# Two message-passing layers on one core: sums over partitions of two groups in four strips, and fewer waits

## The reference

```
h = 2.0 ** 0.5 * relu(emb @ W1 / 10.0 ** 0.5)                 # (E, 16)
w = (h @ W2 / 16.0 ** 0.5).reshape(E, 7, MUL, MOUT)           # 7 weight matrices per edge
s_out, g_out = 8 scalars each, from xs and xv.y1
v_out        = 8 vectors,      from xs, xv and xv.y2
s_act = 1.593 * tanh(s_out); gates = 1.593 * tanh(g_out)
edge_ftr = concat([s_act, gates[:, :, None] * v_out]) * norm[:, None]
return segment_sum(edge_ftr, edge_dst)
```

## Time and profile before

| | us |
|---|---|
| three executions | 5657.39, 5658.57, 5661.72 |
| median | 5658.57 |
| the profiled execution | 5663.47 |
| its span, first to last instruction | 5661.7 |
| message stage in it (first to last `FT` copy) | 416 to 3341 |

### The profile page before, as it was taken

One profiled execution on the slowest core, in us unless ns is written; L12 is line 12 of the kernel. 1 busy time (PEld: TensorE's weight loads), 2 busy tenths in 40 slices (PEclk: granted clock), 3 DMA queues, 4 the chain that ended last, 5 costly groups with the idle time before them and its releaser, 6 DMA issues. The chain is left out here.

```text
span 5661.7 us, 70210 instructions
## 1 busy us (share of the span) xinstructions
PE 4006.7 (71%) x20839; PEld 2129.7 (38%) x20839; DVE 3192.8 (56%) x5351; ACT 1475.9 (26%) x2862; POOL 3379.2 (60%) x3371
## 2 busy tenths in 40 slices
PE   0005888787888888877877860099898998999870
PEld 0002322222222222232222320077666666766650
DVE  4504776776767776677776763044444444455442
ACT  2002444444444444444444430000000000001000
POOL 5675555555555555555555417666666666666756
PEclk9999888888888888888888985599999989999985
DMA  8411111111111111111111101022222222222211
GB/s 300 114 38 18 38 37 36 37 37 37 37 35 33 36 37 31 34 37 37 37 37 37 35 18 22 18 41 45 43 43 43 42 43 43 43 42 48 46 27 24
DMA packets 266652, 252.42 MB, mean 45 GB/s; under 512 B 182208, under 2 KB 236936, under 8 KB 263777
## 3 DMA queue, kind: packets, MB, share of 16 engines
q1 hardware_dynamic: 157028, 174.83, 11.2%
q0 software_dynamic: 109024, 72.30, 9.0%
q10 hardware_dynamic: 462, 4.00, 0.2%
HBM read 160.54 MB, written 90.34 MB: 44 GB/s over the span
## 5 line engine op out<-in xcount | busy, mean ns | idle before, releaser
L612 POOL DMA_INDIRECT edge<-xp_d,idx x1440 | 1421.4, 987 | 1089.0 <-issue 419.4
L864 DVE TENSOR_TENSOR prod<-G_ps,hid 128x1000 f32<-128x1000 f32 x1200 | 1399.4, 1194 | 884.6 <-remote 410.6
L1198 POOL DMA_INDIRECT gxb<-tab_d,idxb x1200 | 1259.1, 1049 | 577.0 <-issue 334.4
L753 PE MATMUL G_ps<-FT,wst 32*128 32x500 f32 x4800 | 999.3, 685 | 362.7 <-DVE prod L864 244.4
L1233 PE MATMUL G_ps<-tb,hot 125*126 125x500 f32 (+1 forms) x3200 | 727.8, 378 | 395.5 <-DVE hotk L1255 301.1
L782 PE MATMUL R_ps<-prod,red 128*32 128x500 f32 x4800 | 923.8, 706 | 0.8 <-ACT rt L678 0.8
L1233 PEld LDWEIGHTS G_ps<-tb,hot 125*126 125x126 f32 x3200 | 572.0, 201 | 537.5 <-issue 446.8
L753 PEld LDWEIGHTS G_ps<-FT,wst 32*128 32x128 f32 x4800 | 270.7, 200 | 827.5 <-DVE prod L864 412.3
L773 PE MATMUL T_ps<-FT,wst 32*128 32x500 f32 x800 | 522.4, 737 | 3.1 <-issue 3.1
L666 ACT ACTIVATE FT<-T_ps 128x500 f32<-128x500 f32 x400 | 235.0, 588 | 856.3 <-PE G_ps L753 629.9
L782 PEld LDWEIGHTS R_ps<-prod,red 128*32 128x32 f32 x4800 | 180.8, 124 | 691.2 <-issue 445.5
(11 more groups left out here) (242 smaller groups left out, 4541.3 us busy)
## 6 DMA issues: line engine op xcount, KB each, us to landing
xd_d<-zeros SPq DMA_DIRECT2D x16, 1562.5 KB
y_d<-zrb SPq DMA_DIRECT2D x40, 595.0 KB
edge<-xp_d,idx POOLq DMA_INDIRECT x1440
xv<-xd_d SPq DMA_DIRECT2D x40, 560.0 KB
y_d<-zr SPq DMA_DIRECT2D x40, 560.0 KB
edge<-sel_d SPq DMA_DIRECT2D x40, 546.9 KB
gxb<-tab_d,idxb POOLq DMA_INDIRECT x1200
em<-in_edge_attr SPq DMA_DIRECT2D x40, 175.0 KB
```

Of the source, the lines that this page charges most:

```text
L612: nc.gpsimd.indirect_dma_start(out=edge_c[:, i, 8:8 + DIM], out_offset=None, in_=xp_d, in_offset=bass.IndirectOffsetOnAxis(col, 0)).then_i ...
L753: return Tn.matmul(G_ps[pair][:, a * 512:a * 512 + GW], wst[rows, r * 128:(r + 1) * 128], FT[k][rows, :], start=True, stop=True)
L864: V.tensor_tensor(prod[k][i][:, :].rearrange("p (a e) -> p a e", a=2), gv, hid[k][:, :].rearrange("p (a e) -> p a e", a=1).broadcast_to([1 ...
L1198: nc.gpsimd.indirect_dma_start(out=gx[h][:, c * T1:(c + 1) * T1], out_offset=None, in_=tab_d, in_offset=bass.IndirectOffsetOnAxis(idx[h][: ...
```

## The change

The sums over partitions are made per piece, not per group. Each of a piece's two groups has six pairs (product tile, half) to be added up; `sum_round` takes them in three rounds of four matmuls, each round filling four strips of 32 rows of `R_ps` (two strips per group). `out_of_R` copies 128 rows once per piece, and `back` makes four transposes of 128 rows per piece where there were eight of 96. `red` gets a third block, `prod` four sets of tiles (until now two), `rt` is one tile. The orders of the three engines around it move: on ScalarE `high` comes a group earlier, tanh and the copy of the sums go once per piece; on VectorE `post(0)` and `post(1)` come one group later and `turned` moves to the other group of the piece; transposes of features take columns alternately. A number of waits that another wait in the same stream implies are left out. On GpSimd the indices are copied per piece, and the wait for five ring slots before the copy is gone; `pace` is as it was.

```diff
-        red = sb("red", [128, 2 * 32])
+        red = sb("red", [128, 3 * 32])
...
-            prod = [[sbt(f"prod{k}_{i}", [128, 2 * GW]) for i in range(3)] for k in range(2)]
-            rt = [sbt(f"rt{k}", [96, GW]) for k in range(2)]
+            prod = [[sbt(f"prod{k}_{i}", [128, 2 * GW]) for i in range(3)] for k in range(4)]
+            rt = sbt("rt", [128, GW])
@@ -603,11 +604,9 @@
-                                if c == 0 and s % PC == 0 and not fixed:
-                                    for q in range(s, s + PC):
-                                        hold(S(f"b_gx{q}"), t * 16 * PW + 16 * PW)
-                                    nc.gpsimd.tensor_copy(idx[:, i:i + C], src_i[:, bass.ds((p + RING) * PW, C)]).then_inc(S("b_ix"), 1)
-                                    hold(S("b_ix"), t * 2 + s // PC - 1)
+                                if c == 0 and not fixed:
+                                    nc.gpsimd.tensor_copy(idx[:, i:i + PW], src_i[:, bass.ds((p + RING) * PW, PW)]).then_inc(S("b_ix"), 1)
+                                    hold(S("b_ix"), p - RING + 1)
@@ -687,11 +681,16 @@
-                            if k == 1 and not (last and g + 3 >= G2):
-                                s = (g + 3) // 2
+                            if k == 0 and not (first and g < 4):
+                                tanh(t * RING + g // 2 - 2)
+                            if k == 0 and not (last and g + 4 >= G2):
+                                s = (g + 4) // 2
                                 high(t * RING + s, s % RING, t * 2 + s // PC)
+                            if k == 1 and not (first and g < 2):
+                                out_of_R(t * RING + g // 2 - 1)
...
+                            if not (last and g == G2 - 1):
+                                relu(n + 1, 1 - k)
                             if not (last and g >= G2 - 2):
                                 out_of_T(n + 2, k)
-                            if k == 1 and not (first and g < 3):
-                                tanh(t * RING + (g - 3) // 2)
-                            if not (last and g == G2 - 1):
-                                relu(n + 1, 1 - k)
-                            if not (first and g == 0):
-                                out_of_R(n - 1, 1 - k)
@@ -772,40 +764,45 @@
-                    def reduce(n, k):
-                        pe.wait_ge(S("b_mul"), n * 3 + 3)
-                        if some(n):
-                            pe.wait_ge(S("b_rt"), n)
-                        for a in range(2):
-                            for o in range(3):
-                                i = (o, (0, 2, 1)[o])[a]
-                                last = Tn.matmul(R_ps[32 * o:32 * o + 32, 0:GW], red[:, a * KF:(a + 1) * KF], prod[k][i][:, a * GW:(a + 1) * GW], start=(a == 0), stop=(a == 1))
-                        last.then_inc(S("b_R"), 1)
...
+                    def sum_round(m, b, u):
+                        if u == 0:
+                            pe.wait_ge(S("b_mul"), m * 6 + 6)
+                            if some(m):
+                                pe.wait_ge(S("b_rt"), m)
+                        for q in range(4):
+                            pair, a = ((0, 0), (1, 0), (2, 0), (0, 1), (2, 1), (1, 1))[q % 2 * 3 + u]
+                            last = Tn.matmul(R_ps[32 * q:32 * q + 32, 0:GW], red[:, u * KF:(u + 1) * KF],
+                                             prod[b * 2 + q // 2][pair][:, a * GW:(a + 1) * GW], start=(u == 0), stop=(u == 2))
+                        if u == 2:
+                            last.then_inc(S("b_R"), 1)
+
+                    def back(m):
+                        pe.wait_ge(S("b_rt"), m + 1)
+                        if some(m):
+                            pe.wait_ge(S("b_yr"), m)
                         pe.sem_inc(S("go"), 1)
                         for c in range(GT):
+                            last = Tn.transpose(Y_ps[0:P, c * 128:(c + 1) * 128], rt[:, c * P:(c + 1) * P], ident[:, :])
                         last.then_inc(S("b_Y"), 1)
@@ -854,17 +852,17 @@
                         if i == 0:
                             dve.wait_ge(S("b_hid"), n + 1)
-                        dve.wait_ge(S("b_G"), n * 2 + (1, 1, 2)[i])
-                        if i == 0 and later(n):
-                            dve.wait_ge(S("b_R"), n - 1)
+                            dve.wait_ge(S("b_G"), n + 1)
+                        if i == 2:
+                            dve.wait_ge(S("b_G2"), n + 1)
...
-                            if k == 0:
-                                q = (g + 4) // 2
+                            if k == 1:
+                                q = (g + 5) // 2
                                 more = not (last and q >= RING)
                                 if more:
                                     turned(t * RING + q, q % RING, t * 2 + q // PC, q % RING // PC, t + q // RING)
...
-                            elif not (first and g < 3):
-                                q = (g - 3) // 2
+                            elif not (first and g < 4):
+                                q = (g - 4) // 2
                                 for i in range(2):
                                     post(i, t * RING + q, q % RING // PC, q % RING % PC, t if q >= 0 else t - 1)
```

More of the change, by code:

```diff
@@ L249, in _ @@
                     nc.gpsimd.memset(edge_c[:, :, SD + 40:EW], 0.0)
-                    for i in range(2):
+                    for i in range(3):
                         blk = red[:, i * KF + i * MO:i * KF + (i + 1) * MO]
@@ L648, in gather_sums @@
                         act.wait_ge(S(f"b_z{h}"), t * NPC + i + 1)
-                        if some(ch):
+                        if i == 0 and some(ch):
                             act.wait_ge(S("b_st"), ch * 32)
@@ L766, in round2 @@
                         product(k, 1, 0, 0, 0)
[L767 removed]
+                        product(k, 1, 1, 0, 1).then_inc(S("b_G2"), 1)
                     def hidden(n, k):
@@ L798, in turn @@
                             g2, p2 = (g + 2) % G2, t * RING + (g + 2) // 2
+                            m, b = t * RING + g // 2 - 1, (g // 2 - 1) % 2
+                            sums_due = not (first and g < 2)
                             round1(n, k)
+                            if sums_due:
+                                sum_round(m, b, 2 * k)
                             if not (last and g >= G2 - 2):
                                 transposes(n + 2, g2, p2)
-                            if not (first and g < 2):
-                                back(n - 2, k)
                             round2(n, k)
@@ L806, in turn @@
                                 hidden(n + 1, 1 - k)
-                            if not (first and g == 0):
-                                reduce(n - 1, 1 - k)
+                            if sums_due and k == 0:
+                                sum_round(m, b, 1)
+                            if sums_due and k == 1:
+                                back(m)
                     transposes(0, 0, 0)
@@ L816, in _ @@
                     turn(PAIRS - 1, last=True)
-                    reduce(NG - 1, 1)
-                    back(NG - 2, 0)
-                    back(NG - 1, 1)
+                    for u in range(3):
+                        sum_round(NPIECES - 1, 1, u)
+                    back(NPIECES - 1)
                 @block.vector
@@ L914, in turn @@
                                 scan = lambda: fill(gc, ch + 1, 1 - h)
[L915 to L920 removed]
+                            if 5 <= gc < 9 and not (first and h == 0):
+                                scan = lambda: sums(gc - 5, ch - 1, 1 - h)
+                            multiply(n, k, b, 0)
+                            multiply(n, k, b, 1)
+                            if k == 1 and not (first and g < 5):
+                                q = (g - 5) // 2
                                 post(2, t * RING + q, q % RING // PC, q % RING % PC, t if q >= 0 else t - 1)
@@ L951, in _ @@
                         fill(i, 0, 0)
-                    for p in range(2):
+                    for p in range(3):
                         turned(p, p, 0, 0, 0)
@@ L958, in _ @@
                     turn(PAIRS - 1, last=True)
-                    post(2, NPIECES - 2, 1, PC - 2, PAIRS - 1)
-                    for i in range(3):
-                        post(i, NPIECES - 1, 1, PC - 1, PAIRS - 1)
+                    for p in range(2):
+                        for i in range(3):
+                            post(i, NPIECES - 2 + p, 1, PC - 2 + p, PAIRS - 1)
                     carry_sums(NCH - 1, 1, PAIRS - 1)
```

77 lines of the change are left out of this document (30 added, 47 removed).

## The result

The changed kernel is slower: 5876.72 us (median of 4, 5875.1 to 5909.66) against 5660.15 for the kernel before on the same chip (5657.39 to 5674.17), a ratio of 1.0391, 95% interval 1.0351 to 1.0432. On another chip it was 1.0392 (1.0362 to 1.0422). The forecast was 5600, its range 5450 to 5800.

A forecast was written before the change was run, and what follows sets the result against it. Loop taken as bound by unbroken gather runs withholding TensorE's messages: 5663.5 - 72 (loop) + 17 (turn 0) - 4 (sums) = 5604.5, median 4.9 lower, so 5600 us; own range 5550 to 5645, full range 5450 to 5800.

The forecast's parts named there:

- The bound: Message loop: how many gathers follow without pause and what TensorE must announce meanwhile; 1.8 of 7.3 us a group.
- `pace` against the new order: GpSimd in the loop: gather 5 never waits again; every piece has six gathers, the copy, two more and one pause.
- The copy's pause, "hidden": GpSimd's index copy per piece: 1.0 us more queue, hidden within 11.0 of 14.2 us; two gathers behind it add 0.4.
- X between 7.18 and 8.69: Time from a six-gather run's first start to the withheld first product; middle taken, period 13.84, 14.2 with 0.4, -72 us.
- The period's other terms: Loop piece after the withheld message: 3.33 us from first product to third, 2.57 from third to next run.
- Nothing moves: Rival, loop: the drain holds round 1 to 8.69 us in every piece, period 14.59; 5662 us, chance 0.20.
- The rival: Two gathers behind the copy prolong the run and hold messages in the loop; 15.2 us a piece, 5779 us, chance 0.25.
- The sums: TensorE's sums in three steps, not four: 0.2 us a group without gathers, 4 us in the last turn.
- Turn 0: First turn, without copies: gathers form runs of eight, draining 2.5 us later in 7 pieces; +17 us.
- Waits left out: Omitted waits were already met earlier in the stream, so worth nothing, between -1 and +1 us.
- The clock: TensorE's granted clock in the loop stays about as now, 0.87.

The follow-up runs named there:

- the three copies: Changed kernel with each index copy made three times in a row, lengthening the pause between gather 7 and gather 0; 5620.93 us, 0.9929 of the kernel before.
- four sets of two: Changed kernel with `pace` waits added and moved so gathers go in four pairs, each behind its own event; 5455.64 us, 0.9628 of the kernel before.

## Why the prediction was wrong, point by point

- *The bound* (a pattern of gathers, not busy time) was right; that TensorE's messages are withheld "until the gathers have drained" was too strong, as the last section shows. Without the gathers the kernel before takes 112.4 us a turn instead of 146.6, near the 109 of its last turn.
- *`pace` against the new order*: right to the letter, six, copy, two in every piece.
- *The copy's pause, "hidden"*: **this step failed.** I priced it as time on GpSimd's queue, where it is indeed hidden, gave the two gathers behind it 0.4 us for which I named no row, and left the question whether 1.3 us (0.99 in the trace after) are long enough for a drain of 1.47 to a rival. They are not. With 1.70 us of pause a piece takes 14.42 us instead of 15.81: 1.4 us, not 0.4, or 250 us in 180 pieces, and by the ratios that run is some 260 us faster.
- *X between 7.18 and 8.69, "I take the middle"*: failed as well. The middle of the period, 13.84, holds an X of 7.94. With the pause long enough X is 8.74, at the end of my range that gave no gain; round 1 first in line did not slip through. One message in the earlier trace rows had carried the whole gain. The period's other terms, 3.33 and 2.57, came out as they were: 8.74 + 3.34 + 2.57 = 14.65, measured 14.42. The two errors together, 0.8 for X and 1.0 for the two gathers, make 16.0 of the 14.2 that I forecast; 15.8 was measured.
- *"Nothing moves", 14.59 as now*: the earlier trace rows and the trace of before could have told that 14.66 was a mean of several kinds. Between 600 and 3200 us, pieces with a pause before gather 2 and one before gather 5 took 13.97 us (71 of them), with the first alone 14.81 (46), with the second alone 15.63 (29, which the expectation above left out), with neither 15.15 (25). That is from gather 2 to gather 2. From gather 0 to gather 0 pieces with both pauses take 14.63 us, with the first alone 14.94, with the second alone 14.36, with neither 14.78, so these lengths do not give the price of a pause. That taking the second one away costs is shown by the kernel before without that wait, 1.0257.
- *The rival* gave 12.2 for X and 14.8 or 18.1 for the period, of which I took 15.2. X is between the two: in 52 of 158 pieces the message comes at 11.6 us, about as this rival had it (11.9 with the pause of 0.99 in place of 1.3), and they take 17.5 us; in the others it comes before the second gather has landed (10.06 in the rows, 0.51 after that gather's start). 15.8 was measured.
- *The sums*: 0.2 us a group, 4 us in the last turn, predicted; 2.2 us measured there (103.7 to 101.5), and 0.24 a group where there are no gathers at all. The two switches of the array's mode more, 0.4 us a piece by my estimate from the earlier trace rows, do not keep this from being a gain: 0.48 us a piece is left. The Trainium skill ("TensorEngine Tiling (Array Packing)", Key Properties) says that a change of tiling mode drains TensorE; how much of the gain that takes no run here tells apart.
- *Turn 0*: +17 predicted, +5.5 measured. *Waits left out*: nothing in the traces speaks against a price of nothing; they were not tried alone.
- *The clock*, "about as now, 0.87": 0.82. It was higher where the stalls were shorter: 0.86 with the three copies, 0.90 with four sets of two, and without gathers 1.00 with the new streams and 0.98 with the old ones.

## What to carry to other kernels

Where one engine's back-to-back transfers hold up what others announce, price each transfer by when the whole run of them drains, and each pause by whether it is longer than the drain: here a pause 0.7 us too short gave back little. A change that leaves the pacing numbers as they are and moves the events they count has changed the pacing: retune it first, then judge the rest. And look for the kinds of cycles in a mean period before you call a forecast "as now", but cut the cycles at more than one place: a kind that is short by one cut can be long by another.

## What was not expected of the hardware

- Two more small operations on GpSimd per piece, some 0.36 us each in its queue, made the kernel some 260 us faster by the ratios (5890.92 and 5620.93, on two chips): the messages of TensorE came through in the 1.70 us pause in 162 of 173 pieces, and in one of 0.99 in 19 of 158.
- A gather that starts before the run ahead has drained puts off the message, but not always by its own drain: X was 8.7 for six, 10.2 in the median for six and two with 0.99 between them, 11.55 for eight.
- The two first gather runs keep VectorE idle as before:

```profile
452.80 1.20 DVE L862 TENSOR_TENSOR prod<-G_ps,hid 128x1000 f32<-128x1000 f32 x1 [18.98 <-remote]
479.47 2.31 DVE L862 TENSOR_TENSOR prod<-G_ps,hid 128x1000 f32<-128x1000 f32 x2 [25.47 <-remote]
```

- Those runs also show that a pause is not needed for a message to come through: in the kernel before 61 gathers follow each other from 397.64 us on with 0.30 us between them, and yet products start at 428.27 and at 449.88 us, in their midst. The row of the first:

```profile
428.27 2.31 DVE L864 TENSOR_TENSOR prod<-G_ps,hid 128x1000 f32<-128x1000 f32 x2 [15.68 <-issue]
```

- Messages between other engines pass while gathers run. In the piece of the changed kernel shown above, beside the last gather of the six, ScalarE starts 0.03 us after the end of the VectorE instruction that it waits for:

```profile
1519.07 0.58 DVE L852 TENSOR_REDUCE edge<-tmp 125x128 f32<-125x384 f32 x1
1519.68 0.94 ACT L656 ACTIVATE HL<-edge 125x384 f32<-125x384 f32 x2 [1.21 <-DVE edge L852]
```

What keeps TensorE's messages back, whether their delivery or something that TensorE itself waits for (the ends of its matmuls are modelled), no run here tells.
